# Five query units of a linear-attention stage: max(x, 0) on ScalarE, min(e^x, 1) on GpSimd, their sum in TensorE's attention product

## The reference

```python
q_p = jax.nn.elu(jnp.einsum('bhnd,hdf->bhnf', q, proj)) + 1.0
k_p = jax.nn.elu(jnp.einsum('bhnd,hdf->bhnf', k, proj)) + 1.0
kv = jnp.einsum('bhnf,bhnd->bhfd', k_p, v)
attn = jnp.einsum('bhnf,bhfd->bhnd', q_p, kv)
k_sum = k_p.sum(axis=2)
z = 1.0 / (jnp.einsum('bhnf,bhf->bhn', q_p, k_sum) + 1e-08)
attn = attn * z[..., None]
```

## Time and profile before

| | |
|---|---|
| median of 3 runs | 482.74 us (482.45 to 485.15) |
| the profiled execution | 483.11 us |
| its span | 481.4 us |
| TensorE, matmul busy | 418.6 us (87%) |
| VectorE busy | 310.0 us (64%) |
| GpSimd busy | 257.0 us (53%) |
| ScalarE busy | 236.5 us (49%) |

### The profile page before, as it was taken

The page is one execution under the profiler, slowest core; times in us unless marked ns, Lnnn a source line. Parts: engine busy times, 40 slices in busy tenths (PEclk is TensorE's granted clock), DMA queues, the critical chain, the costliest instruction groups (busy, mean ns, idle before and its releaser), DMA issues.

```text
span 481.4 us, 8149 instructions
## 1 busy us (share of the span) xinstructions
PE 418.6 (87%) x2850; PEld 304.6 (63%) x2850; DVE 310.0 (64%) x744; ACT 236.5 (49%) x371; POOL 257.0 (53%) x321
## 2 busy tenths in 40 slices
PE   7889795878898899999898999889878979999970
PEld 6534352334697899999864333345347969999960
DVE  4898789999663323415696999899985602431364
ACT  4877755343230354343168988878762204435320
POOL 4899584899678865465305000020556732556470
PEclk9999899787899999999999999999997999999995
DMA  5457580993171232225624434595011121221276
GB/s 143 128 154 291 157 259 27 321 311 109 36 231 50 67 89 61 82 61 206 185 63 104 99 96 99 136 284 186 24 33 46 51 84 40 63 87 58 81 253 203
DMA packets 50328, 60.89 MB, mean 126 GB/s; under 512 B 7152, under 2 KB 29296, under 8 KB 50288
## 3 DMA queue, kind: packets, MB, share of 16 engines
q1 hardware_dynamic: 42672, 47.50, 33.4%
q0 software_dynamic: 4608, 8.47, 5.4%
q10 hardware_dynamic: 3008, 4.40, 2.8%
HBM read 29.78 MB, written 25.31 MB: 114 GB/s over the span
## 4 chain that ended last, share of the span: by engine, by line
PE 38%; DVE 11%; issue 9%; ACT 8%; DMA 6%; POOL 5%; ACTq 1%; POOLq 0%; DVEq 0%; SPq 0%
PE ps L1412 34%; DVE feat L1332 5%; POOL slots_x L517 4%; ACT expo L865 3%; PE ps L1568 2%; DMA xe<-slots_x 2%; DMA last_got<-chosen_y 2%; ACT rows_x L712 1%; DMA chosen_y<-ye,y_to 1%; DMA slots_x<-rows_x,put_at 1%; ACT xnT L610 1%; DVE stats L1064 1%; POOL chosen_y L567 1%; DVE part L1312 1%; DVE xres L1359 1%
## 5 line engine op out<-in xcount | busy, mean ns | idle before, releaser
L567 POOL DMA_INDIRECT chosen_y<-ye,y_to x80 | 79.1, 989 | 67.8 <-DVE ye L1277 49.4
L1332 DVE SCALAR_TENSOR_TENSOR feat<-expo,ps 128x1024 f32<-128x1024 f32 x64 | 75.1, 1214 | 6.3 <-ACT expo L865 6.2
L751 ACT ACTIVATE hT<-ps 128x640 f32<-128x640 f32 x64 | 45.2, 706 | 69.1 <-PE ps L1412 69.1
L517 POOL DMA_INDIRECT slots_x<-rows_x,put_at x64 | 62.8, 980 | 28.8 <-issue 17.7
L865 ACT ACTIVATE expo<-ps,minus_one 128x1024 f32<-128x1024 f32 x64 | 69.9, 1115 | 11.7 <-PE ps L1412 9.6
L1412 PE MATMUL ps<-cproj_sb,hT 128*128 128x128 f32 x640 | 74.6, 275 | 0.3
L1416 PE MATMUL ps<-ident 128*128 128x128 f32 x546 | 68.0, 285 | 7.5 <-DMA slots_x<-rows_x,put_at 4.1
L1412 PEld LDWEIGHTS ps<-cproj_sb,hT 128*128 128x128 f32 x640 | 72.9, 192 | 0.6 <-ACT hT L751 0.6
L1416 PEld LDWEIGHTS ps<-ident 128*128 128x128 f32 x546 | 63.9, 147 | 10.0 <-DMA slots_x<-rows_x,put_at 5.1
L1227 DVE TENSOR_TENSOR xe_low<-ps,xeT 128x640 fp32r<-128x640 f32 x16 | 13.2, 825 | 86.3 <-ACT xeT L610 86.3
L500 POOL TENSOR_TENSOR read<-state,qT 128x512 f32<-128x512 f32 x30 | 38.1, 1276 | 15.1 <-DVE state L1013 14.9
(11 more groups left out here) (238 smaller groups left out, 702.1 us busy)
## 6 DMA issues: line engine op xcount, KB each, us to landing
chosen_y<-empty_rows SPq DMA_DIRECT2D x32, 256.0 KB
decay<-k_rows SPq DMA_DIRECT2D x30, 256.0 KB, 5.1
stk<-part SPq DMA_DIRECT2D x96, 64.0 KB, 2.0
slots_x<-empty_rows SPq DMA_DIRECT2D x16, 325.0 KB, 6.1
xe<-slots_x SPq DMA_DIRECT2D x16, 325.0 KB, 2.9
cfc_sb<-in_L_ffn_c_fc SPq DMA_DIRECT2D x2, 2048.0 KB, 9.8
got<-chosen_y SPq DMA_DIRECT2D x8, 256.0 KB, 5.8
got<-chosen_y ACTq DMA_DIRECT2D x8, 256.0 KB, 7.0
```

Source lines behind the costliest of these rows:

```text
L517: pool.indirect_dma_start(out=slots_x[k], out_offset=bass.IndirectOffsetOnAxis(ap=put_at[:, c, kk, t:t + 1], axis=0), in_=rows_x[:, kk * N ...
L567: pool.indirect_dma_start(out=chosen_y[k], out_offset=bass.IndirectOffsetOnAxis(ap=y_to[:, b, i:i + 1], axis=0), in_=ye[:, b, i * D:(i + 1 ...
L751: act.activation(hT[:, b, f, :].rearrange("p (a n) -> p a n", a=2), ps[:, 2 + 2 * (f % 2):4 + 2 * (f % 2), 0:HALF], ACT.Gelu).then_inc(h_r ...
L1332: dve.scalar_tensor_tensor(out=feat[:, g % 4, :], in0=expo[:, g % 3, :], scalar=1.0, in1=flat(ps[:, pair, :]), op0=ALU.min, op1=ALU.max).t ...
```

## The change

Five of the query units are done in another way: (c, u) = (1,5), (2,4), (2,5), (3,4) and (3,5). Since elu(x) + 1 = max(x, 0) + min(e^x, 1), ScalarE writes max(x, 0) into the unit's buffer of `feat` with a second pass over the PSUM pair (`above`), GpSimd makes min(e^x, 1) in place in the unit's buffer of `expo` (`below`), and `attend` multiplies both by the same `kvl` and lets PSUM add them. VectorE leaves these units out. The semaphore f_ready now counts only the other units (`whole_past`); two semaphores of earlier stages are used again to count the new steps: wbeta_ready those of `above`, sel_made those of `below`. The pair of PSUM banks of such a unit is free after `above`; its buffer of `expo` is free after the attention product of its pair.

```diff
+        halved = [8 * c + u for c in range(1, NB) for u in (4, 5) if c >= 2 or u == 5]
+        whole_past = lambda g: g - sum(NK + v < g for v in halved)
+        halves_past = lambda g: sum(NK + v < g for v in halved)
+        is_halved = lambda g: g - NK in halved
+        above_ready, below_ready = wbeta_ready, sel_made
...
                 c, u = UNIT_AT[n]
-                return f_ready, NK + 8 * c + u + 1
+                g = NK + 8 * c + u
+                if is_halved(g):
+                    return above_ready, 1 + halves_past(g + 1)
+                return f_ready, whole_past(g + 1)
...
                 if n == TB and k and c == 0:
+                    below(NK + halved[3])
+                    below(NK + halved[4])
                     pool.wait_ge(chosen_ready, NB + 2)
...
+            def below(g):
+                pool.wait_ge(f_exp, g + 1)
+                pool.tensor_scalar(expo[:, g % 3, :], expo[:, g % 3, :], 1.0, None, ALU.min).then_inc(below_ready, 1)
...
+            below(NK + halved[0])
             inverse_root(0)
+            below(NK + halved[1])
+            below(NK + halved[2])
             inverse_root(1)
             experts(1)
...
                 act.wait_ge(f_mm, g + 1)
-                if g >= 3:
-                    act.wait_ge(f_ready, g - 2)
+                if is_halved(g - 3):
+                    act.wait_ge(at_mm, (g - 3 - NK) // 2 + 1)
+                elif g >= 3:
+                    act.wait_ge(f_ready, whole_past(g - 2))
                 act.activation(expo[:, g % 3, :], flat(ps[:, pair, :]), ACT.Exp,
                                bias=minus_one[:]).then_inc(f_exp, 1)
+
+            def above(g, pair):
+                act.wait_ge(at_mm, (g - NK - 4) // 2 + 1)
+                act.activation(feat[:, g % 4, :], flat(ps[:, pair, :]), ACT.Relu,
+                               bias=minus_one[:]).then_inc(above_ready, 1)
...
                     feature_exp(NK + 8 * c + u, pair_of(n))
+                    if 8 * c + u in halved:
+                        above(NK + 8 * c + u, pair_of(n))
...
                 c, u = UNIT_AT[n]
-                    feature(NK + 8 * c + u, pair_of(n))
+                    if 8 * c + u not in halved:
+                        feature(NK + 8 * c + u, pair_of(n))
...
                 for w in (v - 1, v):
-                    for x, (gp, a_, cg) in enumerate(two_heads(w % 8)):
-                        ins = mm(ps[32 * cg:32 * cg + 32, 6 + gp, :], kvl[:, gp, a_, cg, :],
-                                 feat[:, (NK + w) % 4, x * BK:(x + 1) * BK], start=a_ == 0, stop=a_ == 1,
-                                 tile_position=(0, 32 * cg))
+                    g = NK + w
+                    parts = [feat[:, g % 4, :]]
+                    if w in halved:
+                        pe.wait_ge(above_ready, 1 + halves_past(g + 1))
+                        pe.wait_ge(below_ready, 1 + halves_past(g + 1))
+                        parts.append(expo[:, g % 3, :])
+                    else:
+                        pe.wait_ge(f_ready, whole_past(g + 1))
+                    for n, part_of in enumerate(parts):
+                        for x, (gp, a_, cg) in enumerate(two_heads(w % 8)):
+                            ins = mm(ps[32 * cg:32 * cg + 32, 6 + gp, :], kvl[:, gp, a_, cg, :],
+                                     part_of[:, x * BK:(x + 1) * BK], start=a_ == 0 and n == 0,
+                                     stop=a_ == 1 and n == len(parts) - 1, tile_position=(0, 32 * cg))
```

More of the change, by code:

```diff
@@ L1867, in _ @@
                     c, u = UNIT_AT[n]
-                    pe.wait_ge(f_ready, NK + 8 * c + u + 1)
+                    if 8 * c + u not in halved:
+                        pe.wait_ge(f_ready, whole_past(NK + 8 * c + u + 1))
                     if c == 0 and u == 1:
@@ L1886, in _ @@
                     keep_warm(8, pair_of(n + 3).start + 1)
-            pe.wait_ge(f_ready, NK + NQ)
+            pe.wait_ge(f_ready, whole_past(NK + NQ))
             keep_warm(8, 5)
```

## The result

The changed kernel takes 488.94 us (median of 4 runs, 486.96 to 492.26), the kernel before 482.60 us beside it (4 runs, 480.67 to 485.15). The ratio is 1.0118, with a 95% interval of 1.0070 to 1.0165: slower by 1.2%, which is 5.7 us (the two medians lie 6.3 us apart). Forecast were 487.7 us, in a range of 483 to 491. The profiled execution of the changed kernel took 488.25 us, with a span of 486.5.

A forecast was written before the change was run, and what follows sets the result against it. The prediction took VectorE to bound the query units; block losses of 1.1, 1.25 to 2.15 and 1.9 to 2.8 us, taken as 5.0, on the median 482.74 gave 487.7 us, range 483 to 491.

The forecast's parts named there:

- VectorE bounds the units: Query units, block 2: VectorE fullest, 13.62 of 14.00 us; five fewer combinations relieve it of at most 5.65 us.
- rival 1: VectorE stays what ends the blocks and its relief of 5.65 us arrives: 477.1 us; chance 0.07.
- Relu: ScalarE's five added 128x1024 passes: 1.1 us each, 1.0 to the next start, delaying the copy at_sb by 1.0 us.
- Minimum: GpSimd's five 128x1024 minima in place: 2.0 us each, bounds 0.23 and 5.0, holding nobody up to 3.8 us.
- Second product: TensorE's added product over expo for a changed unit's pair: 1.4 us, between 0.9 and 1.8.
- The new wait: ScalarE's Exp waits for the attention product to free expo; u = 7 starts t + 7.1 to 8.0, before t + 5.2.
- The sum: Losses of blocks 1 to 3: 1.1 + 1.25 to 2.15 + 1.9 to 2.8 = 4.25 to 6.05 us, taken as 5.0.
- Rival 3, the clock: TensorE's clock falls once more as it waits longer in blocks 2 and 3: about 2 us more, 489.5 us; chance 0.09.
- Rival 2 (GpSimd): GpSimd binds at 5.0 us a minimum, delaying blocks 1 to 3: some 5 us more, about 493 us; chance 0.09.
- rival 4 (hidden): Second products overlap fully, Relu disappears in ScalarE's later waits: 0 to 4 us lost, about 485 us; chance 0.15.
- The tail: Behind the last combination, through block 3's logits to GpSimd's last scatter: unchanged, passing on the 4 to 6 us delay.

The follow-up runs named there:

- e7: Changed kernel with four expo buffers, the five combinations left out and no Relu, minimum or second product instead; ratio 0.9951 to the kernel before.
- e8: Changed kernel with only (2,4) and (3,4) halved, four expo buffers, at_sb copy first, GpSimd adding the halves, one product; ratio 0.9979 to the kernel before.
- e2: Changed kernel with ScalarE's copy at_sb of u = 5 ahead of that unit's Relu, still three expo buffers; 485.39 us, ratio 1.0055 to the kernel before.
- e6: Changed kernel with every GpSimd minimum done twice, one after the other; 502.29 us in one run.
- e5: Changed kernel with GpSimd's minimum over only the first 512 of 1024 columns; 490.43 us, ratio 1.0145 to the kernel before.
- e4: Changed kernel without the second attention product (over expo) of the five units, all waits kept; 486.15 us, ratio 1.0037 to the kernel before.
- e1: Changed kernel with four buffers of expo instead of three, nothing else different; 483.60 us, ratio 0.9992 to the kernel before.
- both edits: Changed kernel with four buffers of expo and the copy at_sb ahead of the Relu; 481.89 us, ratio 0.9981 to the kernel before.

## Why the prediction was right, step by step

- **VectorE bounds the units.** Right as a reading, wrong as a price. The prediction had 5.65 us as the most that can be gained; relief by itself brought 2.4 us. The step that failed took every hole-free stretch of VectorE as one queue. In it stands a step that TensorE's out-projection holds at a fixed distance (e7, e8). The forecast did not rest on this term, rival 1 did: without any new cost the kernel would have come to about 480 us, not 477.1.
- **Relu.** 1.11 to 1.14 us, 1.0 us apart, as forecast. Its place ahead of the copy costs 1.0 us in each of blocks 2 and 3 (e2).
- **Minimum.** Taken as 2.0 us, it is 2.77, inside the bounds of 0.23 and 5.0 and under the 3.8 us from which it was to decide (3.3 by the rows, see e6). Nobody waits for it (e5), and twice the time binds (e6). The Trainium skill's page "GPSIMD Engine Reference", section "Elementwise — side-by-side cycle accounting", led to an estimate of 0.9 to 1.5 us; the trace does not agree, with 2.77 us for 1024 columns and 1.49 for 512.
- **Second product.** Taken as 1.4 us, it is 0.88 us (338.20 to 339.08), the lower bound; e4 gives 0.89 in a block. The eight rows over expo take 1.05 us, those over feat 1.08, and they overlap their neighbours alike. The Trainium skill's page "TensorEngine Tiling (Array Packing)", section "Key Properties" (tiles operate independently), weighed against my middle value, and the trace agrees with it.
- **The new wait.** Right. Counted from t, the Exp of (2,5): transposes of the copy at t + 2.66 (forecast 2.74), product at t + 4.95 (5.04), u = 7 exponential at t + 7.04 (7.1 to 8.0). ScalarE's 3.4 and 3.6 us of idle time and VectorE's 2.3 and 2.4 us were named beforehand. With another buffer 3.2 of the 4.4 us come back that are lost without the clock's fall (e1).
- **The sum.** Block 1 loses 0.91 us (forecast 1.1), block 3 1.90 (1.9 to 2.8), block 2 1.57 without the fall of the clock (1.25 to 2.15) and 2.69 with it. That is 4.4 us without it, 5.5 with it, where 5.0 stood. Without the clock 5.0 is 0.6 us too much, since the second product came out at its lower bound; the clock, which was left out of the sum, added 1.1. That the sum lies so near the measured length is in part luck.
- **Rival 3, the clock,** came in part, in some executions: 1.1 us in block 2, forecast 2. What decides whether it falls stays open; the same waits stood ahead of it where it fell and where it did not. **Rival 2 (GpSimd)** and **rival 4 (hidden)** did not come; in e6, where GpSimd does bind, it cost more than my figures for it, with a clock that fell behind the wait.
- **The tail** behind the last combination is unchanged: 4.6 us later at the logits and at the last landing.

## What to carry to other kernels

When work is taken from one engine and its buffer is then freed by another, later step, price the time the buffer is held before the work that is saved: here one more buffer gave back 3.2 of 4.4 us, the clock left aside. And before relieving the fullest engine, look in its own order for the next step that another engine feeds at a fixed distance; what is relieved ahead of that step is lost in its wait, and what is relieved behind it is kept only up to the engine's next wait (1.06 to 1.16 us in blocks 2 and 3, 0.19 in block 1).

## What the runs showed of the hardware

- GpSimd's minimum with a constant reads one tile and is slower than its sum of two: 128x1024 in place takes 2.77 us, the sum of two tiles of that shape 2.37 us. From 512 to 1024 columns the minimum grows by 1.28 us, so 2.5 ns a column and 0.2 us beside.
- A second set of eight 512-column products on the same column groups, over other data, costs 0.88 us: the sixteen take 1.9 us, the eight took 1.06. The second unit's rows over feat start 0.03 us behind the first unit's (338.23 and 338.20), though the first unit's product over expo stands between them in TensorE's list: column groups don't wait for each other's rows here.
- A minimum on GpSimd makes a step of VectorE longer. In all nine kernels with the minimum over 1024 columns the four 128x1 steps `hit` of blocks 2 and 3 take 1.21 to 1.23 us together, the first of them 0.82 to 0.84; beside the minimum over 512 columns 0.79 to 0.80; without a minimum (before, e7) 0.61, each 0.21 to 0.22. The addition to the residual beside the minimum keeps its 0.69 us. No run shows what in the minimum holds them.
- The time of the first 300 us varies by up to 5.5 us between these traces, as much as the change itself; TensorE's clock early on has a part in it. The table by stretch, first of the kernel with the copy first, then of the one with both edits:

```profile
0.00:100.00 100.00, 85.13 (x324) 0.86 0.57 178
```

```profile
0.00:100.00 100.00, 82.28 (x346) 0.91 0.61 193
```

The first query exponential starts at 300.68 us in the one and 295.15 in the other. Such runs are compared by stretches within their traces.
